# GpSimd's order in the batch turns: the first half's multiply ahead of the eight gathers of the next batch's second tile

## The chip, the cores and the metric

One core of a Trainium2 chip runs the whole program. The metric is device microseconds (us) of one execution; "before" is the median of three runs. The engines are TensorE (PE in the rows; PEld are its weight loads), VectorE (DVE), ScalarE (ACT), GpSimd (POOL) and SyncE (SP, which here only issues DMAs). Each runs its own instructions in order and waits on semaphores that the others raise.

## The reference, cut to what matters

Sixteen batches of 256 tokens of width 256 go through one decoder layer of three parts, each with a residual and a layer norm. Only the first two touch the change.

```python
# 1: memory of 8192 keys, top 8 per token
Q = x @ shared_compress[b];  scores = Q @ K.T / sqrt(128)
topk_scores, topk_idx = top_k(scores, 8);  weights = softmax(topk_scores)
x = layernorm(x + sum_k V[topk_idx[k]] * weights[k])
# 2: cross-attention, 16 heads of 64
q = x @ Wq;  k, v = split(context @ Wkv)
attn = softmax(clip(where(mask, q @ k.T / 8, -max), -5, 5))
x = layernorm(x + (attn @ v) @ Wo + bo)
# 3: routed feed-forward over groups of 32 tokens, once, after all batches
```

The eight rows V[topk_idx[k]] of 128 tokens (one tile) are fetched by eight gathers, one for each k. The softmax is divided late: attn @ v is made from unnormalised exponentials and multiplied by the inverse of the denominators.

## The kernel before, in words

All loops are written out at build time, so the order on each engine is fixed; `need(engine, semaphore, value)` is a wait. After a preamble the program goes through turns, `for c in TURNS`. Turn c does the attention of batch c (`cross`), the values V of batch m = c + 1 (`mid`), the scores against the keys of batches up to c + 2 (`score`, one block of 512 keys each, spread between everything else), and the output of batch p = c - 1 (`out`).

On TensorE a turn runs: the K projections (four jobs, `("K", c, j)`) with scores between them; the output product (`("WO", p, tile)`, `qT_heads` times `wo`); the transposes of x1 of tile 1; the Q projections; then, head pair by head pair, similarities (`sims`), `values` (`("PV", c, j)`, `exp` times `v`) and, after each half of the heads, `denominators` (`exp` times `head_selector`, into `den`). The turn ends with the four V projections of batch m (`("V", m, j)`, in the rows `side_bank<-wqkv_hi,ctx_hi` and its two companions), with a score block after each, and the transposes of x1 of tile 0 of batch m (line 548). The projection jobs use two PSUM banks in turn: a job needs the job two before it copied out by ScalarE (`heads_out`, line 927). I call the stretch from the first V matmul to the transposes of line 548 the V stretch.

The denominators of half h travel so: VectorE inverts `den` (`den_inverse`, line 1225), SyncE stores the result to DRAM (line 366 in the issue rows) and reads it back broadcast into `kT` (line 370, semaphore `rb_in0` or `rb_in1`), and GpSimd multiplies `qT_heads` (attn @ v of that half) by it: line 1446, semaphore `ot_done`. Two wait for that: ScalarE, before it copies the next batch's K jobs into `kT` (jobs 0 and 1 need the first half, 2 and 3 the second), and TensorE, before the output product (both).

On GpSimd a turn runs: small layer norm work, the gathers of tile 0 of batch m (five in a row, then one and two among the clips), the clips of `exp` (line 1425), and at its end the part that changes: gathers of tile 1 of batch m (`v_rows`, line 1397) and the two multiplies. VectorE sums the gathered rows of tile 1 (`value_sum`, line 1200) early in the next turn, before the transposes of x1 of tile 1.

Of the kernel before, what the change touches and what calls it, by code (L numbers as in the profile page):

```python
# [22 lines left out]
TOPK = 8  # L23
# [61 lines left out]
def build(nc, x, xT, xTs, ctxT, mcol, A, AT, BmT, WimpT, WrT, comp, KmT, V, Wq, Wk, Wv, Wo, bo, ctrl, f1, fb, f2,  # L85
# [4 lines left out]
    with ExitStack() as ctx:  # L90
        names = {}

        def sem(name):
            if name not in names:
                names[name] = ctx.enter_context(nc.semaphore(name))
            return names[name]
# [149 lines left out]
        def need(eng, name, v):  # L246
            if v > 0:
                eng.wait_ge(sem(name), v)
# [8 lines left out]
        def job_full(eng, key):  # L257
            need(eng, f"proj_full{JOB[key] % 2}", JOB[key] // 2 + 1)

        def job_done(eng, key):  # L260

            need(eng, f"proj_free{JOB[key] % 2}", JOB[key] // 2 + 1)
# [1114 lines left out]
        @block.gpsimd  # L1377
        def _(pool):

            for n in range(NK // KW):  # L1380
                pool.wait_ge(sem("k_hi"), n + 1)
                ks = slice(n * KW, (n + 1) * KW)
                nc.gpsimd.tensor_tensor(kl[:, ks], kraw[:, ks], kh[:, ks].bitcast(F32), ALU.subtract)\
                    .then_inc(sem("k_lo"), 1)

            pool.wait_ge(sem("main_ready"), 1)
            for n, (w, i, k) in enumerate(WCHUNKS):
                pool.wait_ge(sem("w_hi"), n + 1)
                nc.gpsimd.tensor_tensor(wl[:, i, k, :], wraw[:, 1, i, k, :], wh[:, i, k, :].bitcast(F32),
                                        ALU.subtract).then_inc(sem("w_lo"), 1)  # L1390

            def gather(batch, tile, ks):
                if ks[0] == 0:
                    need(pool, "sum_done", TT * batch + tile)
                    need(pool, "idx_done", TT * batch + tile + 1)
                for k in ks:
                    pool.indirect_dma_start(out=vg[:, k, :], out_offset=None, in_=V_rows,  # L1397
                                            in_offset=bass.IndirectOffsetOnAxis(ap=i8[:, tile, k:k + 1], axis=0))\
                        .then_inc(sem("vg_in"), 16)

            def rstd1(batch, tile):
                need(pool, "sum_done", TT * batch + tile + 1)
                nc.gpsimd.tensor_tensor(rs[:, tile:tile + 1], ve[:, tile:tile + 1], neghalf[:, 0:1], ALU.pow)\
                    .then_inc(sem("rstd1"), 1)

            for c in TURNS:
                m, a, p = c + 1, c + 2, c - 1
                cross, mid, out = (0 <= b < B for b in (c, m, p))
                if cross:
                    rstd1(c, 1)  # L1410
                    need(pool, "x1T_pe", TT * (c + 1))
                    for tile in range(TT):
                        last = nc.gpsimd.tensor_tensor(x1[c % 2][:, tile, :], x1[c % 2][:, tile, :], bob[:, :], ALU.add)
                    last.then_inc(sem("bo_done"), 1)
                if mid:
                    gather(m, 0, range(0, 5 if cross and m < B - 1 else TOPK))
                if out:
                    need(pool, "sum2_done", p + 1)
                    nc.gpsimd.tensor_tensor(rs2[:, :], ve2[:, :], neghalf[:, :], ALU.pow).then_inc(sem("rstd2"), 1)
                for h in range(H):  # L1420
                    if cross:
                        i = H * c + h
                        need(pool, "exp_done", i + 1)
                        for k in range(KT):
                            last = nc.gpsimd.tensor_scalar(ex[i % NEX][:, k, :], ex[i % NEX][:, k, :], ub[:, k, c:c + 1],  # L1425
                                                           E_LO, ALU.min, ALU.max)
                        last.then_inc(sem("clip_done"), 1)
                    if cross and m < B - 1 and h == 1:
                        gather(m, 0, (5,))
                    if cross and m < B - 1 and h == 3:  # L1430
                        gather(m, 0, (6, 7))
                    if mid and h == 5:
                        need(pool, "ctx_hi", m + 1)
                        nc.gpsimd.tensor_tensor(ctl[:, :, :], ct[:, :, :], cth[:, :, :].bitcast(F32), ALU.subtract)\
                            .then_inc(sem("ctx_lo"), 1)
                    if mid and h == 9:
                        rstd1(m, 0)
                if mid:
                    gather(m, 1, range(0, 5))
                for half in range(2):  # L1440
                    if cross and 2 * c + half < 2 * B - 1:
                        need(pool, f"rb_in{half}", 32 * (c + 1))
                        job_done(pool, ("PV", c, 2 * half))
                        job_done(pool, ("PV", c, 2 * half + 1))
                        hs = slice(4 * half, 4 * half + 4)
                        nc.gpsimd.tensor_tensor(qt[:, hs, :], qt[:, hs, :], kt[:, hs, :], ALU.mult)\  # L1446
                            .then_inc(sem("ot_done"), 1)
                    if mid and half == 0:
                        gather(m, 1, range(5, TOPK))


            job_full(pool, ("WO", B - 1, TT - 1))
            for j in range(NQ // 2):
                need(pool, "ffn2_pe", j - NF + 1)
                pool.dma_start(f1q[j % NF][:, :, :], f1[:, :, 2 * j * P:2 * (j + 1) * P]).then_inc(sem(f"fq_in{j % NF}"), 16)
                pool.dma_start(f2q[j % NF][:, :, :], f2_t[j]).then_inc(sem(f"fq_in{j % NF}"), 16)

            for n in range(NT):
                u = n % U
                need(pool, "aggr3", n + 1)  # L1460
                need(pool, "out_done", n - U + 1)
                nc.gpsimd.tensor_scalar(ve3[u][:, :], ag3[u][:, 1:2], EPS, None, ALU.add).then_inc(sem("var3"), 1)
                need(pool, "var3", n + 1)
                nc.gpsimd.tensor_tensor(rs3[u][:, :], ve3[u][:, :], neghalf[:, 0:1], ALU.pow).then_inc(sem("rstd3"), 1)
# [61 lines left out]
```

## Time and profile before

| | |
|---|---|
| time before, median of 3 runs (lowest to highest) | 1380.46 us (1378.34 to 1381.36) |
| the profiled execution: its time, its span | 1377.7 us, 1375.8 us |
| busy share of the span: PE, DVE, POOL, ACT | 96%, 82%, 53%, 52% |
| granted TensorE clock, mean | 0.99 |
| turns that change | those with `cross` and `mid`: c = 0 to 14 |

A turn takes some 69 us (the gathers at a turn's end start at 532.09, 601.19, 669.91 us). TensorE is busy nearly all the time, so the question for a change on GpSimd is where TensorE waits for something that comes from GpSimd's place in the order. The timeline rows below give for each instruction its start, its duration, engine, line, operation, result<-inputs, sizes, count, and in brackets the idle time before it and who ended it.

### The profile page before, as it was taken

The page shows a single profiled execution, that of the slowest core. Times are in us where ns is not written, and L with a number is a line of the kernel's source. Part 1 is how long each engine was busy: PE and PEld are TensorE (multiplying, and loading weights), DVE is VectorE, ACT ScalarE, POOL GpSimd, SP SyncE. Part 2 cuts the span into 40 slices and gives each one's busy share as a digit, 9 for nine tenths or more (in the row PEclk, how much of TensorE's full clock was granted, in tenths as well). Part 3 has the DMA queues.
Part 4 walks back from the last instruction along what each step waited for, and adds up shares of the span by engine and source line. Part 5 has one row for each costly group of instructions (what it writes and reads, how often), then busy time and mean ns, then how long its engine had stood idle before and what let it go on. Part 6 is the DMA issues. An engine that isn't in the chain of part 4 may idle for free.

```text
span 1375.8 us, 25304 instructions
## 1 busy us (share of the span) xinstructions
PE 1321.6 (96%) x9877; PEld 993.5 (72%) x9877; DVE 1125.4 (82%) x1628; ACT 718.8 (52%) x1377; POOL 728.9 (53%) x1009
## 2 busy tenths in 40 slices
PE   9877999999999999999999999999999999999898
PEld 5455778786878787878787868787878676767775
DVE  2479889898989898989898988898989986546567
ACT  1353655555555555555555555555555544336554
POOL 0554465555565656565655565656565647341434
PEclk9997999999999999999999999999999999999999
DMA  9562121212121212121212121212121216002412
GB/s 368 182 197 65 46 74 54 74 55 74 54 74 55 74 54 74 55 74 54 74 54 74 54 74 54 74 55 74 54 74 44 74 42 182 1 26 84 156 43 83
DMA packets 57557, 110.38 MB, mean 80 GB/s; under 512 B 9446, under 2 KB 38110, under 8 KB 56286
## 3 DMA queue, kind: packets, MB, share of 16 engines
q1 hardware_dynamic: 40350, 62.17, 15.0%
q0 software_dynamic: 14848, 41.96, 10.6%
q10 hardware_dynamic: 2240, 4.63, 0.9%
q8 instruction: 79, 1.29, 0.4%
q14 instruction: 40, 0.33, 0.1%
HBM read 98.50 MB, written 10.22 MB: 79 GB/s over the span
## 4 chain that ended last, share of the span: by engine, by line
PE 88%; DVE 5%; issue 2%; another core or an unknown queue 2%; ACT 2%; DMA 0%; SPq 0%; POOL 0%; POOLq 0%; ACTq 0%; DVEq 0%
PE side_bank L387 51%; PE score_bank L387 33%; PE score_bank L766 2%; DVE cand_idx L1177 1%; DVE cand_val L1174 1%; PE side_bank L766 1%; DVE dispatchedT L1335 1%; PE side_bank L548 1%; ACT exp L922 0%; PE score_bank L606 0%; ACT score_row L910 0%; SPq L318 0%; DVE x_sum L1200 0%; POOL exp L1425 0%
## 5 line engine op out<-in xcount | busy, mean ns | idle before, releaser
L910 ACT COPY score_row<-score_bank 128x512 f32<-128x512 f32 x512 | 298.9, 591 | 112.2 <-PE score_bank L387 56.7
L1397 POOL DMA_INDIRECT v_rows<-in_V,top_idx x256 | 249.0, 973 | 130.8 <-issue 74.5
L1174 DVE MAX8 cand_val<-score_row 128x8 f32<-128x2048 f32 x128 | 291.7, 2279 | 28.6 <-ACT score_row L910 26.3
L1177 DVE FIND_INDEX8 cand_idx<-cand_val,score_row 128x8 uint32<-128x2048 f32 x128 | 292.5, 2285 | 0.0
L1425 POOL TENSOR_SCALAR exp<-exp,exp_bound 128x256 f32<-128x256 f32 x512 | 248.9, 502 | 79.8 <-ACT exp L922 78.1
L387 PE MATMUL score_bank<-keysT_hi,qT_hi 128*128 128x512 f32 x512 | 216.9, 424 | 21.0 <-ACT score_row L910 19.9
L387 PE MATMUL score_bank<-keysT_hi,qT_lo 128*128 128x512 f32 x512 | 204.9, 400 | 0.0
L387 PE MATMUL score_bank<-keysT_lo,qT_hi 128*128 128x512 f32 x512 | 204.7, 400 | 0.0
L922 ACT ACTIVATE exp<-side_bank 128x512 f32<-128x512 f32 x256 | 139.1, 595 | 91.3 <-PE side_bank L387 84.3
L387 PE MATMUL side_bank<-qT_heads,kT 64*128 64x256 f32 x1024 | 145.2, 402 | 2.6 <-ACT exp L922 2.6
L387 PEld LDWEIGHTS score_bank<-keysT_hi,qT_hi 128*128 128x128 f32 x512 | 97.9, 191 | 62.1 <-ACT score_row L910 25.3
L1200 DVE SCALAR_TENSOR_TENSOR x_sum<-v_rows,top_weight,x_sum 128x256 f32<-128x256 f32 x256 | 134.2, 524 | 9.1
L927 ACT COPY qT_heads<-side_bank 128x512 f32<-128x512 f32 x128 | 75.2, 587 | 113.9 <-PE side_bank L387 91.9
L387 PE MATMUL side_bank<-exp,v 128*64 128x256 f32 x1024 | 125.5, 386 | 1.1 <-POOL exp L1425 1.0
L387 PEld LDWEIGHTS side_bank<-qT_heads,kT 64*128 64x128 f32 x1024 | 88.2, 186 | 51.5 <-issue 41.3
L387 PE MATMUL side_bank<-wo,qT_heads 128*128 128x256 f32 x512 | 115.8, 379 | 0.0
L387 PEld LDWEIGHTS score_bank<-keysT_hi,qT_lo 128*128 128x128 f32 x512 | 97.6, 191 | 23.9
L1446 POOL TENSOR_TENSOR qT_heads<-qT_heads,kT 128x1024 f32<-128x1024 f32 x31 | 74.4, 2399 | 71.2 <-DMA kT<-den_scratch 70.9
L387 PEld LDWEIGHTS score_bank<-keysT_lo,qT_hi 128*128 128x128 f32 x512 | 98.1, 192 | 15.7
L387 PEld LDWEIGHTS side_bank<-wo,qT_heads 128*128 128x128 f32 x512 | 96.7, 190 | 15.0 <-issue 1.2
L1225 DVE RECIPROCAL den_recip<-score_bank 128x256 f32<-128x256 f32 x32 | 56.0, 1749 | 60.4 <-remote 51.5
L387 PEld LDWEIGHTS side_bank<-exp,v 128*64 128x64 f32 x1024 | 67.4, 136 | 51.0 <-issue 20.9
(200 smaller groups left out, 2284.0 us busy)
## 6 DMA issues: line engine op xcount, KB each, us to landing
kT<-den_scratch SPq DMA_DIRECT2D x62, 256.0 KB
f_quads<-in_f POOLq DMA_DIRECT2D x32, 256.0 KB, 3.4
comp_then_wqkv_raw<-in_comp SPq DMA_DIRECT2D x6, 1024.0 KB, 19.0
xT_by_step<-in_xTs SPq DMA_DIRECT2D x4, 1024.0 KB, 9.1
xT_in<-in_xT SPq DMA_DIRECT2D x16, 256.0 KB
keysT_raw<-in_KmT ACTq DMA_DIRECT2D x8, 512.0 KB, 20.2
x_sum<-in_x SPq DMA_DIRECT2D x32, 128.0 KB, 2.0
ctxT_in<-in_ctxT SPq DMA_DIRECT2D x16, 256.0 KB
```

Source lines behind the costliest of these rows:

```text
L387: return nc.tensor.matmul(o, l, r, start=start, stop=stop, skip_group_check=True)
L766: last = nc.tensor.transpose(set2[n % 3][:, c0:c0 + P], dtt[:, n, k, :, g], idn[:, :])
L910: nc.scalar.copy(srow[n // PER % 2][:, i * CB:(i + 1) * CB], scb[n % 3]).then_inc(sem("score_evac"), 1)
L922: nc.scalar.activation(ex[i % NEX][:, :, :].rearrange("p k s -> p (k s)"), sp_[o][:, :], ACT.Exp, scale=A_SCALE).then_inc(sem("exp_done"), 1)
L927: nc.scalar.copy(to, job_bank(key)[:, :]).then_inc(free(key), 1)
L1174: own(nc.vector.max(cv[:, tile, cs], srow[g % 2][:, :]))
L1177: nc.vector.max_index(ci[:, tile, cs], cv[:, tile, cs], srow[g % 2][:, :]).then_inc(sem("cand_done"), 1)
L1200: own(nc.vector.scalar_tensor_tensor(acc[:, tile, :], vg[:, k, :], w8[:, tile, k:k + 1], acc[:, tile, :], ALU.mult, ALU.add))
L1225: nc.vector.reciprocal(rden[:, :], den).then_inc(sem("rden_done"), 1)
L1397: pool.indirect_dma_start(out=vg[:, k, :], out_offset=None, in_=V_rows, in_offset=bass.IndirectOffsetOnAxis(ap=i8[:, tile, k:k + 1], axis=0))\
L1425: last = nc.gpsimd.tensor_scalar(ex[i % NEX][:, k, :], ex[i % NEX][:, k, :], ub[:, k, c:c + 1], E_LO, ALU.min, ALU.max)
L1446: nc.gpsimd.tensor_tensor(qt[:, hs, :], qt[:, hs, :], kt[:, hs, :], ALU.mult)\
```

## The change

In turns with `cross` and `mid`, GpSimd ran five gathers of tile 1, the multiply of the first half, three gathers, the multiply of the second half. Now it runs the multiply of the first half, all eight gathers, the multiply of the second half. In the turn that has `mid` without `cross` (c = -1) the eight gathers stay in a row as they were.

```diff
@@ -1435,8 +1435,8 @@
                     if mid and h == 9:
                         rstd1(m, 0)
-                if mid:
-                    gather(m, 1, range(0, 5))
+                if mid and not cross:
+                    gather(m, 1, range(TOPK))
                 for half in range(2):
                     if cross and 2 * c + half < 2 * B - 1:
                         need(pool, f"rb_in{half}", 32 * (c + 1))
@@ -1445,8 +1445,8 @@
                         nc.gpsimd.tensor_tensor(qt[:, hs, :], qt[:, hs, :], kt[:, hs, :], ALU.mult)\
                             .then_inc(sem("ot_done"), 1)
-                    if mid and half == 0:
-                        gather(m, 1, range(5, TOPK))
+                    if mid and cross and half == 0:
+                        gather(m, 1, range(TOPK))
```

The end of turn 1 on GpSimd before, from the last clip on:

```order
103 L1425 TENSOR_SCALAR exp<-exp,exp_bound 128x256
104 L1397 DMA v_rows<-in_V,top_idx 128x256 [waits idx_done,sum_done]
105 L1397 DMA v_rows<-in_V,top_idx 128x256 x4
106 L1446 TENSOR_TENSOR qT_heads<-qT_heads,kT 128x1024 [waits proj_free1,proj_free0,rb_in0]
107 L1397 DMA v_rows<-in_V,top_idx 128x256 x3
108 L1446 TENSOR_TENSOR qT_heads<-qT_heads,kT 128x1024 [waits proj_free1,proj_free0,rb_in1]
109 L1403 TENSOR_TENSOR ln_rstd<-ln_var,neghalf 128x1 [waits sum_done]
```

And the same place of the changed kernel:

```order
102 L1425 TENSOR_SCALAR exp<-exp,exp_bound 128x256
103 L1446 TENSOR_TENSOR qT_heads<-qT_heads,kT 128x1024 [waits proj_free1,proj_free0,rb_in0]
104 L1397 DMA v_rows<-in_V,top_idx 128x256 [waits idx_done,sum_done]
105 L1397 DMA v_rows<-in_V,top_idx 128x256 x7
106 L1446 TENSOR_TENSOR qT_heads<-qT_heads,kT 128x1024 [waits proj_free1,proj_free0,rb_in1]
107 L1403 TENSOR_TENSOR ln_rstd<-ln_var,neghalf 128x1 [waits sum_done]
```

Five gathers moved from ahead of the first multiply, with its wait on `rb_in0`, to behind it; the other engines' orders are the same as before.

## Rows read from the trace of the kernel before

**Rows 1.** The page, the chain that ended last, by engine

```profile
PE 88%; DVE 5%; issue 2%; another core or an unknown queue 2%; ACT 2%; DMA 0%; SPq 0%; POOL 0%; POOLq 0%; ACTq 0%; DVEq 0%
```

**Rows 2.** Waits, whole run: total us, times, longest

```profile
PE side_bank L387 <- ACT v L927: 2.3, 3, 1.1
...
PEld side_bank L387 <- ACT v L927: 5.0, 7, 1.5
...
ACT v L927 <- remote: 69.1, 14, 6.0
...
DVE den_recip L1225 <- remote: 51.5, 15, 4.3
```

**Rows 3.** Timeline, TensorE: V stretch begins and ends, turns 0, 8, 13

```profile
192.16 0.50 PE L387 MATMUL side_bank<-wqkv_hi,ctx_hi 128*128 128x512 f32 x1
...
200.81 0.38 PE L548 MATMUL side_bank<-identity,x 128*128 128x128 f32 x2
...
742.34 0.50 PE L387 MATMUL side_bank<-wqkv_hi,ctx_hi 128*128 128x512 f32 x1
...
750.82 0.38 PE L548 MATMUL side_bank<-identity,x 128*128 128x128 f32 x2
...
1086.89 0.50 PE L387 MATMUL side_bank<-wqkv_hi,ctx_hi 128*128 128x512 f32 x1
...
1096.69 0.38 PE L548 MATMUL side_bank<-identity,x 128*128 128x128 f32 x2
```

**Rows 4.** Timeline, GpSimd, end of turn 6

```profile
601.19 1.03 POOL L1397 DMA_INDIRECT v_rows<-in_V,top_idx  x1 [0.16 <-issue]
...
606.30 0.96 POOL L1397 DMA_INDIRECT v_rows<-in_V,top_idx  x1 [0.30 <-issue]
607.28 2.40 POOL L1446 TENSOR_TENSOR qT_heads<-qT_heads,kT 128x1024 f32<-128x1024 f32 x1
...
612.41 0.96 POOL L1397 DMA_INDIRECT v_rows<-in_V,top_idx  x1 [0.30 <-issue]
619.02 2.40 POOL L1446 TENSOR_TENSOR qT_heads<-qT_heads,kT 128x1024 f32<-128x1024 f32 x1 [5.64 <-DMA kT<-den_scratch]
```

**Rows 5.** Turn 6: denominators on the chain, then timeline of VectorE, ScalarE

```profile
602.88 1.86 PE score_bank L387 x32
...
608.45 1.76 DVE L1225 RECIPROCAL den_recip<-score_bank 128x256 f32<-128x256 f32 x1 [3.16 <-remote]
...
608.52 0.59 ACT L927 COPY v<-side_bank 128x512 f32<-128x512 f32 x1 [5.00 <-remote]
```

**Rows 6.** Timeline, after the second multiply: ScalarE, VectorE, TensorE twice

```profile
621.45 0.59 ACT L927 COPY kT<-side_bank 128x512 f32<-128x512 f32 x1 [2.73 <-POOL qT_heads L1446]
...
621.47 4.13 DVE L1200 SCALAR_TENSOR_TENSOR x_sum<-v_rows,top_weight,x_sum 128x256 f32<-128x256 f32 x8
...
622.18 0.45 PE L387 MATMUL side_bank<-wo,qT_heads 128*128 128x256 f32 x1
...
630.55 0.27 PE L548 MATMUL side_bank<-identity,x 128*128 128x128 f32 x1
```

**Rows 7.** DMA queues within 599 to 605 us: packets, MB, share

```profile
q1 hardware_dynamic: 314, 0.66, 42.5%
q0 software_dynamic: 92, 0.26, 15.0%
```

**Rows 8.** Timeline, SyncE's issue of the second half's broadcast, turn 6

```profile
612.67 1.61 SPq L370 DMA_DIRECT2D kT<-den_scratch  x2
```

**Rows 9.** Turn -1, eight gathers in a row: GpSimd, TensorE, ScalarE

```profile
134.15 0.95 POOL L1397 DMA_INDIRECT v_rows<-in_V,top_idx  x1 [0.30 <-issue]
...
133.31 0.63 PE L387 MATMUL side_bank<-wqkv_hi,ctx_lo 128*128 128x512 f32 x1
...
133.98 0.59 ACT L927 COPY v<-side_bank 128x512 f32<-128x512 f32 x1 [1.97 <-PE side_bank L387]
```

**Rows 10.** Turn 14, beside the eight gathers of tile 0: ScalarE

```profile
1129.52 0.59 ACT L927 COPY qT_heads<-side_bank 128x512 f32<-128x512 f32 x1 [3.23 <-remote]
```

## The prediction

> **What bounds the kernel now.** I read the page's chain first: 88% of it is TensorE [rows 1]. So a change on GpSimd counts only where TensorE waits, and the next view is the list of waits. It has one entry at the place of the change: TensorE waits for ScalarE's copies of the V jobs, 2.3 us in three turns by its matmuls, 5.0 us in seven turns by its weight loads [rows 2]. Those copies themselves wait 69.1 us, and VectorE's inverse of the denominators 51.5 us, both with a releaser the profile cannot name ("remote") [rows 2].
>
> To price the entry I measured the V stretch of turns 0 to 13 in the timeline. It holds the same matmuls each time, so its shortest length is the one without a wait. In turn order the fourteen are 8.65, 8.48, 9.37, 8.47, 8.48, 8.47, 8.78, 8.64, 8.48, 9.34, 8.48, 8.66, 8.48 and 9.80 us; the rows show turns 0, 8 and 13 [rows 3]. The sum over 8.47 is 4.0 us, between the 2.3 and the 5.0 of the list of waits. Turn 14 has no scores in its V stretch, and no wait of TensorE on those copies; it is left out.
>
> Why the copies are late is seen in turn 6. The denominators' matmuls are over at 602.88 + 1.86 = 604.74 us, but VectorE, idle, starts the inverse at 608.45, and ScalarE starts the V copy at 608.52 [rows 5]. Two engines with different waits are let go together, 1.2 us after the fifth gather (606.30 + 0.96 = 607.26) [rows 4]. I found this distance, 1.1 to 1.3 us from the start of the first multiply to ScalarE's copy, in all fourteen turns from 0 to 13. So I take it that news of finished matmuls doesn't get through while this row of gathers runs. That is a reading of coincidence, not something a row states.
>
> **The change part by part.** Nothing is removed or added: eight gathers and two multiplies in each of 15 turns, in another order. In turn 6:
>
> 1. First multiply. The clips end at 601.0 (0.16 before the first gather) [rows 4]. It must then wait for its broadcast. The 512 KB broadcast and a 128 KB row load are 0.66 MB together, and the hardware queue had moved 0.66 MB by 605.0, even beside two gathers [rows 7]. So it runs by 605.0 to 607.4 (2.40 us) instead of 607.28 to 609.68. Behind its wait stand the gathers, for at most 4 us; they have no one who is waiting yet.
> 2. Denominators. They end at 604.74 with no gather issued. If my reading holds, VectorE inverts as soon as it is free, at about 605.3 (608.45 less its idle 3.16) to 607.1, instead of 608.45 to 610.21 [rows 5]. ScalarE copies V when its matmuls end. The wait of TensorE goes: 4.0 us in fourteen turns, bounds 2.3 and 5.0.
> 3. Gathers. From 607.6, spaced as before: five take 6.07 us from start to end, each further one 1.26, so eight take 9.9 and end at 617.5, where the last ended at 613.37 [rows 4]. That is 4.1 us later. What they serve is the sum on VectorE, which started at 621.47, and then the transposes of tile 1 at 630.55 [rows 6]. So the rows have 4.0 us to land before the sum would even start late, and from its start to the transposes are 9.1 us, of which it takes 4.13. No cost. If the cover were gone (a landing some 3 us after 621.5), each further us would hold the transposes by as much.
> 4. Second broadcast. The inverse was over at 610.21, the broadcast issued at 612.67, the multiply let go at 619.02: 2.46 and 6.35 us [rows 4, 5, 8]. From 607.1 on this gives 609.5 and 615.9. One or two more gathers share the engines than before; two cost 15.0% of 6 us, 0.45 us each [rows 7]. So 616.4 to 616.8, still ahead of the last gather.
> 5. Second multiply. Released by the gathers, not by the broadcast: 617.7 to 620.1, against 621.42 before. ScalarE's third K copy waited 2.73 us for it and ran at 621.45, and the output product came at 622.18 directly after the matmuls ahead of it [rows 6]. So there is no wait of TensorE to win there, but 1.3 us more room. What is late next is the gathers themselves, and they have that room.
> 6. After it, VectorE is about 1 to 2 us ahead at the start of each turn. It is not what TensorE waits for, so I count 0 (0 to 0.6 us over the run).
>
> Sum: 0 - 4.0 + 0 + 0 + 0 - 0 = -4.0 us, bounds -2.3 and -5.6. Against the profiled execution (1377.7 us, span 1375.8) that is 1373.7. That execution is 2.8 us faster than the median of the runs shown, 1380.46; taken from the median the sum gives 1376.5 us (1374.9 to 1378.2).
>
> The worst point is 2 together with 3: now eight gathers run in a row beside the V and K projections. The nearest rows are the eight gathers of turn -1, also beside V jobs. There the copy started at 133.98, 0.04 us after its matmuls (133.31 + 0.63), with seven gathers of the row issued and the eighth about to be, at 134.15 [rows 9]. That speaks for no late news with these matmuls. Against it stand the eight gathers of turn 14 beside the similarities: ScalarE waited 3.23 us, again "remote" [rows 10]. The similarities and the denominators are matmuls over a part of the array, and the V and K projections use all of it (128*128). In all cases where the news was late a part-array matmul came first; I rest on that.
>
> The Trainium skill, page "SBUF — State Buffer", section "Who interferes with whom", says that only VectorE and GpSimd contend, that TensorE and ScalarE never wait on anyone, and that DMA contends with no compute engine. By that rule gathers can't hold back ScalarE's copy, what holds it is something else that the change leaves in place, and the sum would be 0 instead of -4.0.
>
> **The rivals.**
>
> A. The forecast: late releases in the V stretch go. 1376.5 us. Chance 0.60.
>
> B. The change doesn't do what it could: what lets VectorE and ScalarE go late hangs on the denominators' matmuls or on something else at that place, and moves with them. For it: the releaser is unnamed, and in turns 9 and 13 VectorE was let go before ScalarE, not together with it. Against it: the fixed distance to the fifth gather. Then TensorE waits as before, 1380.5 us. Chance 0.25.
>
> C. Slower: the longer row of gathers delays news of the V and K matmuls too. If it is held from 3.6 us into the row (604.74 against 601.19 in turn 6) to 1.2 us after it, that is 611.2 to 618.7. TensorE has two banks, so it would run on until the first K job, which needs the third V copy: about 9.1 us into the V stretch, 613.8. It would stand until 618.7 and a copy of 0.59 us, 5 us a turn, 14 turns: 70 us, 1450 us. If only one copy in a turn is late by the 1.2 us seen after a row, 17 us: 1397 us. It decides from 0.29 us a turn (4.0 / 14). For it speaks the late copy of turn 14 [rows 10], against it the prompt one of turn -1 [rows 9]. Chance 0.13.
>
> The remaining 0.02 is for a gather or broadcast that lands too late (steps 3 and 4).
>
> **How the numbers follow.** A and B hold 0.85. A's own range is 1374.9 to 1378.2, with 1.5 us on each side for a median of runs that lie 3 us apart: 1373.5 to 1379.5. B with the same 1.5 us reaches 1382. The range 1373.5 to 1382 leaves out C and a little of A. A difference of 0.2% is 2.8 us, about what a measurement of this kernel can tell from no change: A gives 0.54 for faster and 0.06 for same, B 0.25 for same, C 0.13 for slower, the rest 0.02 slower.
>
> **What would show it.** Right: VectorE's inverse and the V copies no longer wait for "remote" at a turn's end; V stretches all near 8.47 us; the first multiply waits for its broadcast and the second directly follows the eighth gather; no wait of ScalarE's K copy on GpSimd, or one under 1 us. Wrong: TensorE waiting for copies of V or K jobs beside the eight gathers (C), or the inverse still 3 us late with no gather before it (B). The weakest step is 2, the cause of the late release.

## The result and the profile after

| | before | after |
|---|---|---|
| median of six runs each, us (lowest to highest) | 1378.39 (1375.81 to 1381.36) | 1393.4 (1389.54 to 1397.8) |
| ratio, 95% interval | | 1.0108 (1.009 to 1.0126) |
| profiled execution: time, span, us | 1377.7, 1375.8 | 1391.56, 1389.7 |

The change makes the kernel 1.1% slower. Three more runs of the kernel before bring its median from 1380.46 to 1378.39 us. The span of the profiled executions grew by 13.9 us. The page's chain of work that ended last, by engine, for the changed kernel; the share of TensorE was 88% in [rows 1], ScalarE's 2%:

```profile
PE 85%; DVE 5%; ACT 3%; another core or an unknown queue 3%; issue 2%; DMA 0%; SPq 0%; POOL 0%; POOLq 0%; ACTq 0%; DVEq 0%
```

The waits of the whole run, in the columns of [rows 2]: total us, times, longest us.

```profile
ACT v L927 <- PE side_bank L387: 70.1, 52, 2.9
...
ACT kT L927 <- remote: 48.4, 15, 4.4
...
DVE den_recip L1225 <- PE score_bank L387: 17.8, 14, 5.4
...
PEld side_bank L387 <- ACT kT L927: 13.9, 10, 1.9
...
PE side_bank L387 <- ACT kT L927: 9.7, 9, 1.5
...
PEld side_bank L387 <- ACT exp L922: 6.2, 11, 0.6
```

The two entries that the change was to remove are gone: neither the V copies nor VectorE's inverse waits for "remote" any more. In their place the K copies do, 48.4 us in 15 times, and TensorE waits for them. I call the stretch from the transposes of line 548 to the first matmul of the output product the K stretch, and that from the first shared q matmul (`xT_in,sc_in`) to the first `exp,v` matmul the q stretch. Measured in the timeline as the V stretch was:

| sum over the turns, us | before | after | difference |
|---|---|---|---|
| V stretches, 14 turns (shortest 8.47 and 8.49) | 122.6 | 118.9 | -3.7 |
| K stretches, 14 turns (shortest 8.72 and 8.73; after, up to 10.49) | 122.4 | 135.5 | +13.1 |
| q stretches, turns 1 to 13 (shortest 6.08) | 79.7 | 81.6 | +2.0 |
| the rest between turn 0's V stretch and turn 14's | | | -0.8 |
| ahead of turn 0's V stretch; from turn 14's on | | | -1.1; +4.4 |

Turn 6 shows the whole course. Timeline of GpSimd:

```profile
607.61 2.39 POOL L1446 TENSOR_TENSOR qT_heads<-qT_heads,kT 128x1024 f32<-128x1024 f32 x1 [3.44 <-DMA kT<-den_scratch]
610.16 1.05 POOL L1397 DMA_INDIRECT v_rows<-in_V,top_idx  x1 [0.16 <-issue]
...
619.10 0.96 POOL L1397 DMA_INDIRECT v_rows<-in_V,top_idx  x1 [0.30 <-issue]
620.08 2.38 POOL L1446 TENSOR_TENSOR qT_heads<-qT_heads,kT 128x1024 f32<-128x1024 f32 x1
```

VectorE and ScalarE in the same turn:

```profile
608.34 1.74 DVE L1225 RECIPROCAL den_recip<-score_bank 128x256 f32<-128x256 f32 x1
...
609.76 0.59 ACT L927 COPY v<-side_bank 128x512 f32<-128x512 f32 x1 [2.85 <-PE side_bank L387]
...
617.65 0.37 ACT L914 CAST x1T_hi<-side_bank 128x256 fp32r<-128x256 f32 x1 [0.30 <-PE side_bank L548]
...
622.00 0.59 ACT L927 COPY kT<-side_bank 128x512 f32<-128x512 f32 x1 [3.98 <-remote]
```

And TensorE:

```profile
608.07 0.50 PE L387 MATMUL side_bank<-wqkv_hi,ctx_hi 128*128 128x512 f32 x1
...
616.56 0.38 PE L548 MATMUL side_bank<-identity,x 128*128 128x128 f32 x2
...
618.09 0.28 PE L387 MATMUL side_bank<-ctx_hi,wqkv_lo 128*128 128x256 f32 x1
...
622.64 0.39 PE L387 MATMUL side_bank<-ctx_hi,wqkv_hi 128*128 128x256 f32 x1 [1.44 <-ACT kT L927]
...
626.99 3.61 PE L387 MATMUL side_bank<-wo,qT_heads 128*128 128x256 f32 x16
```

The inverse starts 0.3 us into the V stretch, and up to 6.0 us into the row of gathers ScalarE copies each V job within 0.2 us of its matmuls' end. The copy of the transposes at 617.65 already starts 0.7 us behind them (616.56 + 0.38 = 616.94). Then the first K job's matmuls are over at 618.09 + 0.28 = 618.37 us, but its copy starts at 622.00: 1.9 us behind the last gather (619.10 + 0.96 = 620.06). The third K job needs its bank and stands until 622.64, 1.44 us. The K stretch takes 626.99 - 616.56 = 10.4 us instead of 8.7. In the order of before the row of five had ended early in the V stretch (607.26 us in turn 6 [rows 4]), and in the row of three behind it no V or K copy was late.

The trace also holds the time of each semaphore update, from which the views tell a releaser ("remote": the update is there, but no instruction that makes it ended just before). In this turn four groups of matmuls are over at 618.37, 619.07, 620.50 and 621.20 us; their updates come at 621.92, 621.97, 622.10 and 622.15. In the same turn of the kernel before, with the row of five, ends at 604.75, 606.34, 607.04 and 608.44 us have updates at 608.42, 608.50, 608.55 and 608.62. So it isn't ScalarE or VectorE that wakes late: TensorE's updates themselves come late and in one burst. Some updates of these stretches are missing from the record, so nothing is said here of those of other engines. This is what "news" means below.

How far into a row this begins differs. With the row of five ahead of the first multiply, a job that was over 2.4 us after the first gather was held (turn 13); in the rows of eight of the changed kernel none before 6.2 us. Of the fifteen late K copies eleven start 1.6 to 1.9 us behind the last gather and four within 0.3 us of it.

Turn 14 has the same in another place. TensorE, then ScalarE, then the last two of the eight gathers; the row began at 1171.20:

```profile
1181.84 1.10 PE L387 MATMUL score_bank<-x2T_pair,controller 128*128 128x256 f32 x4 [2.56 <-issue]
```

```profile
1181.15 0.59 ACT L934 COPY x2T_pair<-score_bank 128x512 f32<-128x512 f32 x1 [2.96 <-remote]
```

```profile
1178.84 0.95 POOL L1397 DMA_INDIRECT v_rows<-in_V,top_idx  x1 [0.30 <-issue]
1180.09 0.95 POOL L1397 DMA_INDIRECT v_rows<-in_V,top_idx  x1 [0.30 <-issue]
```

Behind the stand of 2.56 us TensorE is slower for a while. Its granted clock was 1.00 (2.4 GHz) up to 1182.9 us and 0.50 (1.2 GHz) from 1184 to 1186, where the 128x256 matmuls take 0.41 us instead of 0.28; from 1187 on it is 1.00 again. From the transposes of line 548 to the output product turn 14 takes 14.19 us instead of 9.85, which is nearly all of the +4.4 at the end of the table.

### The profile page after: what moved, and what is told of

Its sections match the earlier page's. It is cut to its first block, busy times and chain, and to the rows that moved or that the text cites. A ratio compares the mean times of both kernels' runs of the same rounds, so it can differ in the third digit from the quotient of the medians.

```text
span 1389.7 us, 25304 instructions
## 1 busy us (share of the span) xinstructions
PE 1323.9 (95%) x9877; PEld 994.1 (72%) x9877; DVE 1112.0 (80%) x1628; ACT 721.4 (52%) x1377; POOL 726.7 (52%) x1009
## 3 DMA queue, kind: packets, MB, share of 16 engines
q0 software_dynamic: 14848, 41.96, 10.4%
## 4 chain that ended last, share of the span: by engine, by line
PE 85%; DVE 5%; ACT 3%; another core or an unknown queue 3%; issue 2%; DMA 0%; SPq 0%; POOL 0%; POOLq 0%; ACTq 0%; DVEq 0%
PE side_bank L387 49%; PE score_bank L387 32%; PE score_bank L766 2%; DVE cand_idx L1177 1%; DVE cand_val L1174 1%; ACT exp L922 1%; PE side_bank L766 1%; DVE dispatchedT L1335 1%; ACT score_row L910 1%; PE side_bank L548 1%; PE score_bank L606 0%; ACT kT L927 0%; SPq L318 0%; ACT v L927 0%
## 5 line engine op out<-in xcount | busy, mean ns | idle before, releaser
L927 ACT COPY qT_heads<-side_bank 128x512 f32<-128x512 f32 x128 | 75.2, 587 | 103.6 <-PE side_bank L387 92.1
L387 PE MATMUL side_bank<-ctx_hi,wqkv_hi 128*128 128x256 f32 x256 | 76.0, 297 | 10.7 <-ACT kT L927 9.7
```

The source lines that it names most:

```text
L387: return nc.tensor.matmul(o, l, r, start=start, stop=stop, skip_group_check=True)
L927: nc.scalar.copy(to, job_bank(key)[:, :]).then_inc(free(key), 1)
```

## The experiments

The eighteen runs fell on six chips; each group below that shares a chip says so. The kernel before had medians of 1377.8 to 1379.0 us on five of them (on one it is a single run) and 1370.6 on the sixth, so a time is read beside its own chip's. Theories: **T**, news of finished matmuls is held only once a plain-float32 matmul (the transposes) has run beside the gathers; **P**, only part-array matmuls or transposes cause it; **L**, the length of an unbroken row of gathers does it, with **L1** (any compute instruction of GpSimd ends a row) and **L2** (the gathers must pause for about a microsecond); **H**, a broadcast into `kT` beside the gathers does it; **N**, the number of gathers in the last 10 us does.

**First group, one chip (before: 1378.18 us).** The transposes moved ahead of the V jobs, on TensorE and in ScalarE's copies:

```diff
+                if mid:
+                    x1_transpose(m, 0)
                 for j in range(4):
                     if mid:
                         key, tile, hf = ("V", m, j), j // 2, j % 2
...
-                if mid:
-                    x1_transpose(m, 0)
```

> The changed kernel, with the transposes of x1 of tile 0 (line 548) and ScalarE's copy of them moved from behind the V projections to ahead of them, so that between the first of the eight gathers and 1.7 us after the last TensorE runs only projections and scores. Theory T (news of finished matmuls is held back only once a matmul on plain float32 operands has run beside a row of gathers; the transposes are the first such matmul, 6 us into the row): the late K copies go (the 48.4 us in 15 times of ScalarE's K copy behind 'remote' falls under 10), the 13 us of longer K stretches go, time 1377 to 1380 us. Rival L (the length of the row alone holds the news back from its fifth or sixth gather on, whatever matmul runs): K copies as late as before this edit, time 1390 to 1396 us.

Measured 1388.74 us, ratio 1.0082 (1.0062 to 1.0102). Waits:

```profile
ACT kT L927 <- remote: 31.6, 11, 4.7
```

With the transposes over before the row begins, K copies are late eleven times, in ten turns, instead of fifteen times in fourteen turns. T wanted almost none, so the transposes aren't the condition; L wanted them as late as before, and the time is 1.3 us under its range. Why fewer turns are hit I can't say.

Five gathers between the multiplies and three behind the second:

```diff
-                    if mid and cross and half == 0:
-                        gather(m, 1, range(TOPK))
+                    if mid and cross:
+                        gather(m, 1, range(0, 5) if half == 0 else range(5, TOPK))
```

> The changed kernel, but five of the eight gathers between the two multiplies and three behind the second. The row of five starts 2 us into the V stretch and ends at about 8 us, before the transposes; the three run beside the K projections. Theory T: no late news, or only that of the transposes and first K copy for under 1 us; K stretch under 8.9 us; time 1375 to 1380 us. Rival L: rows of five were held up before (the V copies), so the copies of the fourth V job are late from 3.6 us into the row, V or K stretch longer by up to 1 us, time 1380 to 1390 us.

Measured 1400.05 us, ratio 1.0152 (1.0122 to 1.0183). The V stretches are all 8.49 us and the K stretches all 8.73: cutting the row at the same place, beside the same matmuls, took away the whole +13.1. That is against L as it was put here, which had V or K copies late from 3.6 us into a row of five; and the time is above both forecasts. A new wait appears, ahead of the Q projections:

```profile
DVE x_sum L1200 <- DMA v_rows<-in_V,top_idx: 62.5, 15, 5.2
...
PEld side_bank L387 <- DVE x1T_lo L1218: 22.4, 14, 2.4
```

The second multiply waits for its broadcast, the three gathers wait behind it, and the sum of the rows comes so late that the transposes of tile 1 and the Q projections stand, 18.2 us in 14 turns. It is the case that step 3 of the prediction had priced as "if the cover were gone".

Two plain-float32 matmuls behind the third V job, and as a control the same two with fp32r operands; they write a bank that the next score block overwrites, so the output is that of the changed kernel:

```diff
+                    if cross and mid and j == 2:
+                        for _ in range(KT):
+                            mm(sp_[1][:, 0:P], idn[:, :], idn[:, :])
```

> The changed kernel with two extra full-array 128x128 matmuls on plain float32 operands (identity times identity, into an unused bank) in each turn behind the third V job and its scores, 6.3 us into the V stretch and 4.2 us into the row of gathers. They add 0.2 us a turn by themselves. Theory T: from them on the news is held back, so the copy of the fourth V job (in time until now) becomes late in nearly all turns by 3 us or more, and TensorE waits longer: K stretch longer by 1 to 2 us a turn, time 1405 to 1420 us. Rival P (only matmuls over a part of the array or transposes start it): as the changed kernel, 1391 to 1397 us. Rival L: as the changed kernel too.

> The same two extra matmuls at the same place, but on float32r operands (weights of the projection times themselves), as the control. Theory T: no effect beyond 0.1 to 0.2 us a turn; fourth V copy in time, 1391 to 1398 us. If the extra matmuls as such are what matters, it equals the run with the float32 ones.

One run each: 1403.45 and 1394.85 us. The waits of the run with float32:

```profile
ACT v L930 <- PE side_bank L387: 84.6, 59, 2.9
...
ACT kT L930 <- remote: 46.0, 14, 5.4
```

No V copy waits for "remote" with a float32 matmul two jobs ahead of it and gathers all around. The K copies wait as in the changed kernel (46.0, and 47.8 us in the control). The V stretch is longer by the dummies themselves, 0.44 and 0.22 us; over 14 turns the first is 6 us, most of what puts 1403.45 above the forecasts of P and L. T has fallen. P isn't touched by these two runs; against it stands the first of this group, where the row of eight and what followed it had neither transposes nor part-array matmuls beside them until the copies were late.

**Second group, another chip (before: 1378.54 us).** Now the order of before with a shorter first row:

```diff
                 if mid:
-                    gather(m, 1, range(0, 5))
+                    gather(m, 1, range(0, 3))
...
-                        gather(m, 1, range(5, TOPK))
+                        gather(m, 1, range(3, TOPK))
```

> The order of before with three gathers of tile 1 ahead of the first multiply instead of five, and five behind it. Theory L (an unbroken row of GpSimd gathers holds back the news of finished matmuls from some 5 us into the row until 1.2 to 1.9 us behind its end, whatever matmuls run; a break by a multiply lets it through): the row of three ends before the denominators do, the inverse and the V copies go on time, V stretches all 8.48 us; the row of five behind the multiply holds nothing that TensorE waits for (the run with five gathers between the multiplies showed none in the V and K stretches), K stretches 8.73; 1374.5 to 1377.5 us. Theory H (the transfer of a broadcast into kT beside the gathers holds the news): the first half's broadcast still runs beside gathers, V stretches as before, 1377 to 1380 us.

The same with four and four:

> The order of before with four gathers ahead of the first multiply and four behind it. L: the row of four ends 1.2 us earlier than that of five, so the inverse and the V copy go some 1.2 us earlier or on time; of the 4.0 us that TensorE lost in the V stretches at most 1 stays, K stretches 8.73; 1374.5 to 1377.5 us. H: as before, 1377 to 1380 us.

Measured 1376.31 us, ratio 0.9986 (0.9976 to 0.9996), and 1375.66 us, ratio 0.998 (0.9971 to 0.999). In both all V stretches are 8.49 and all K stretches 8.73 us. The waits for the inverse, first with three ahead, then with four:

```profile
DVE den_recip L1225 <- PE score_bank L387: 25.3, 17, 5.1
```

```profile
DVE den_recip L1225 <- remote: 37.4, 15, 4.3
```

With four the inverse is still late (51.5 us in [rows 2]), but let go early enough that the V copies don't cost TensorE anything. So what the change was to win could be had by moving one or two gathers instead of five, and H doesn't fit: the broadcast still lies beside gathers. Both gain less than the 4.0 us, since the q stretches are longer by 2.0 and 1.8 us (more on them below).

The changed kernel without the broadcast of the second half:

```diff
-                        for o in range(2):
+                        for o in range(2 - 2 * h):
...
-                        need(pool, f"rb_in{half}", 32 * (c + 1))
+                        if half == 0:
+                            need(pool, f"rb_in{half}", 32 * (c + 1))
```

> The changed kernel without the broadcast of the second half's inverse into kT, and without GpSimd's wait for it; the second multiply then takes what stands in kT, so that the division of the second half is left out. The eight gathers stay in a row beside the V and K matmuls, as in turn -1, which has no broadcast and no late copy. L: nothing changes, ScalarE's K copies wait 40 to 50 us for remote, 1390 to 1395 us. H: the K copies are on time (under 10 us for remote), K stretches 8.73, 1377 to 1381 us.

One run, 1393.64 us; `ACT kT L927 <- remote` 43.4 us in 13 times, K stretches up to 10.66 us. H has fallen: the late K copies need no broadcast.

Six gathers between the multiplies, two behind:

> The changed kernel with six gathers between the two multiplies and two behind the second. L, with news held from about 5.5 us into a row: the row of six lasts 7.3 us and ends at 615, so at most the third V copy or a score copy is late, V stretches up to 9 us, K stretches 8.73; the two gathers behind the second multiply end about 1.3 us earlier than the three of the run with five between, and part of its 15 us before the Q projections stays: 1385 to 1396 us. H: K copies late as in the changed kernel, and the wait before the Q projections too: over 1400 us.

One run, 1383.08 us. V 8.49, K 8.73 in every turn: a row of six in that place still costs TensorE nothing (two K copies are late, 6.1 us), and of the wait ahead of the Q projections 4.4 us are left. The stretches are as L has them; the time is 1.9 us under its range.

**Third group, another chip (before: 1379.01 us).** The changed kernel with one tiny copy in the middle of the row:

```diff
+        spare = sb(main, "spare", [P, 1])
...
-                        gather(m, 1, range(TOPK))
+                        gather(m, 1, range(0, 4))
+                        nc.gpsimd.tensor_copy(spare[:, :], neghalf[:, 0:1])
+                        gather(m, 1, range(4, TOPK))
```

> The changed kernel with one small GpSimd copy (128x1) of a constant into a spare tile between the fourth and the fifth of the eight gathers; nothing else differs. Theory L1: any GpSimd compute instruction ends the row and lets the news through, so the row of eight becomes two of four: V stretches 8.49, K stretches 8.73, ScalarE's K copies wait under 10 us for remote, 1377 to 1381 us. Theory L2: it takes a pause of the gathers of a microsecond or more (as behind every row so far, 1.2 to 1.9 us from its end to the late copies), so a copy of a fraction of a microsecond changes nothing: K copies wait 40 to 50 us for remote, 1389 to 1395 us.

Measured 1390.19 us, ratio 1.0096 (1.0062 to 1.013); K copies wait 47.9 us in 16 times for "remote". L1 has fallen: a compute instruction as such doesn't end a row.

Four and four, and tile 0's row cut as well:

```diff
-                    gather(m, 0, range(0, 5 if cross and m < B - 1 else TOPK))
+                    gather(m, 0, range(0, 4 if cross and m < B - 1 else TOPK))
...
-                        gather(m, 0, (5,))
+                        gather(m, 0, (4, 5))
```

> The run with four gathers ahead of the first multiply and four behind it, and in turns 0 to 13 also the row of five gathers of tile 0, beside the first similarities, cut to four: the fifth goes behind the second head's clip with the sixth. L (either form): late copies beside the row of five cost 0.2 us a turn in the stretch from the Q projections to the first values (6.08 us at its shortest, 6.3 in most turns); they go in nearly all turns, 2 to 2.7 us less than the run with four and four, 1372 to 1375 us. If the length of the row is not what holds the news, that stretch stays at 6.3 us in most turns and the time at 1375 to 1376.5 us.

Measured 1371.61 us, ratio 0.9953 (0.9938 to 0.9968): 0.5% faster than the kernel before beside it, and 0.4 us under L's range. Thirteen turns, counted from V stretch to V stretch, take 68.53 us each, with no stretch over its shortest; the q stretches are all 6.08 us. The news isn't always in time even so: the inverse waits 36.0 us for "remote" in 14 times beside the row of four, at no cost to TensorE.

**Fourth group, another chip (before: 1377.81 us).** Six and twelve tiny copies in the place of the one, into a spare tile of 12 columns:

> The changed kernel with six of the small copies, one behind the other, between the fourth and the fifth gather, a pause of 0.4 to 1.2 us (one took 0.20 us). L2 (held news gets through once the gathers pause for a microsecond or so): part of the K stretches is near 8.73, the sum of their excess over 8.73 (13.4 us in the changed kernel, 16.8 with one copy) falls to 3 to 10 us; 1379 to 1388 us. L1 (any break does) has fallen. Theory N, a rival: the pause has nothing to do with it and only the number of gathers in the last 10 us counts: excess of the K stretches as with one copy, 12 to 17 us, 1387 to 1393 us.

> Twelve small copies in the same place, a pause of 0.8 to 2.4 us. L2: K copies on time but for those that wait for the second multiply, which now runs up to 2.4 us later (some 622.5 instead of 620.1 in turn 6; the third K copy can wait up to 1 us for it): the excess of the K stretches falls under 4 us, none of it by remote; 1376 to 1382 us. N: excess 12 us or more as before, 1387 to 1395 us.

One run each: 1372.09 and 1369.53 us, with `ACT kT L928 <- remote` at 18.1 us in 8 times and 1.6 us in one; the pauses were 0.78 and 1.48 us. The late copies fit L2, but both times lie some 7 us under its ranges: the shortest stretches had changed too (V 8.43, K 8.52), and the wider tile had moved what lies behind it. Two things had changed at once.

**Fifth group, another chip (before: 1370.58 us)**, to tell these apart. One copy with the wide spare tile; the kernel before with that tile unused; twelve copies timed; the best order with that tile unused:

> The changed kernel with one small copy between the fourth and the fifth gather, as in the first run of this kind, but with the spare tile 12 columns wide as in the runs with six and twelve copies, so that all tiles behind it lie where they lay there. If the pause is what freed the K copies: they are late as with one copy (40 to 50 us for remote, K stretches 10 to 17 us in excess), 1382 to 1391 us. Theory A, that the place of the tiles in SBUF did it: K copies on time, 1369 to 1373 us.

> The kernel before, with the unused spare tile of 12 columns in the place it has in the other runs, and no other change. It gives what the moved tiles are worth by themselves: the shortest stretches were 8.43, 8.52, 11.30 and 8.24 us with six and twelve copies against 8.49, 8.73, 11.34 and 8.34 before. If the place does that, some 0.4 us a turn and 1371 to 1375 us; if not, 1378 to 1380 us.

> The changed kernel with twelve small copies once more, timed. By its one look 1369 to 1371 us, 0.5 to 0.7% under the kernel before.

> The kernel with four and four gathers of tile 1, and tile 0's row cut to four (1371.6 us), with the spare tile of 12 columns and no copies. If the two effects add up: 1371.6 less 4 to 6 us for the shorter stretches, 1365 to 1368 us. If the place of the tiles does nothing: 1371 to 1373 us.

Measured, in that order: 1365.43 us, ratio 0.9961 (0.9945 to 0.9976); 1363.77 us, 0.9949 (0.9934 to 0.9964); 1373.15 us, 1.0017 (1.0008 to 1.0027); 1364.33 us, 0.9955 (0.9942 to 0.9969). The waits of the second of them, the order of before:

```profile
ACT v L928 <- PE side_bank L388: 77.3, 64, 2.9
...
ACT kT L928 <- PE side_bank L388: 52.0, 63, 0.9
...
DVE den_recip L1226 <- PE score_bank L388: 27.9, 14, 5.4
```

On this chip there is no wait for "remote" in any of the four runs, beside rows of five or of eight; V copies, K copies and inverse go when their matmuls end. None of TensorE's 1219 semaphore updates in any of these four traces comes more than 0.12 us behind its matmuls. The expectation that copies would be late with one small copy missed, and the twelve copies took 1373 us instead of 1369 to 1371; but the fourth group had the wide tile and late copies, so it isn't the tile.

Either the chip differs, or something of the one session in which all four ran; the unpadded kernel before, 7 to 8 us faster here than on the other five, fits a chip without held news, but it left no trace here. The gathers keep the same pace, 1.28 us from start to start on either kind of chip. Where no news is held the new order has nothing to win: with one copy it is 1.7 us slower than the order of before with the same tile (1365.43 against 1363.77).

What the tile itself does is a price of its own: -6.8 us against the kernel before beside it. The mean matmul is shorter; groups by shape, before (the first trace, of another chip) and then with the tile (busy us, mean ns):

```profile
L387 PE MATMUL side_bank<-ctx_hi,wqkv_hi 128*128 128x256 f32 x256 | 74.0, 289 | 0.0
...
L387 PE MATMUL side_bank<-wqkv_hi,ctx_hi 128*128 128x512 f32 x128 | 53.5, 418 | 2.3 <-ACT v L927 2.3
```

```profile
L388 PE MATMUL side_bank<-ctx_hi,wqkv_hi 128*128 128x256 f32 x256 | 72.6, 284 | 0.0
...
L388 PE MATMUL side_bank<-wqkv_hi,ctx_hi 128*128 128x512 f32 x128 | 51.7, 404 | 0.0
```

The 418 ns are of a kernel with late V copies; in the two orders of four and four, without the tile, it is 407 and 411. An undisturbed turn takes 68.08 us with the tile and 68.53 without; 14 turns of 0.45 are 6.3 of the 6.8. The shortest K stretch was 8.51 or 8.52 in all runs with the wide tile (three chips) and 8.72 or 8.73 in all others that have a turn without a late K copy, so this goes with the place of the tiles. Why another place makes these matmuls shorter isn't shown. And twelve copies cost here: with no news to free, they only make the second multiply late.

**Last pair, a sixth chip (before: 1378.57 us).** One and twelve copies, same tiles, same chip:

> The same kernel as pad_filler (one copy, spare tile of 12 columns), now side by side with the one of twelve copies on one chip. On a chip on which the rows of gathers hold the news: K copies late for remote by 40 to 50 us, K stretches 10 to 17 us in excess of 8.52, some 1380 to 1386 us with the kernel before at 1378. On a chip like that of pad_before and pad_filler, where not one wait for remote is left: 1365 us, with the kernel before at 1370.6, and nothing is told of the pause.

> The kernel of filler12 and filler12b again. On a chip that holds the news, if the pause of 1.48 us frees it: remote waits of the K copies under 5 us, K stretches under 4 us in excess, 1369 to 1375 us, and 8 us or more under the one with one copy. If the pause does nothing, both have the same time within 3 us and the same late copies. On the other kind of chip 1373 us, for the late second multiply.

Measured 1390.51 us, ratio 1.0097 (1.0068 to 1.0126), and 1375.49 us, ratio 0.9977 (0.9966 to 0.9988). Waits with one copy, and turn 6 on GpSimd and ScalarE:

```profile
ACT kT L928 <- remote: 43.9, 18, 3.9
```

```profile
607.61 1.05 POOL L1398 DMA_INDIRECT v_rows<-in_V,top_idx  x1 [0.16 <-issue]
...
612.46 0.20 POOL L1452 COPY spare<-neghalf 128x1 f32<-128x1 f32 x1
...
616.60 0.95 POOL L1398 DMA_INDIRECT v_rows<-in_V,top_idx  x1 [0.30 <-issue]
```

```profile
619.06 0.59 ACT L928 COPY kT<-side_bank 128x512 f32<-128x512 f32 x1 [0.96 <-remote]
```

The same with twelve:

```profile
ACT kT L928 <- POOL qT_heads L1447: 40.3, 15, 4.1
...
PE side_bank L388 <- ACT kT L928: 3.3, 3, 1.3
```

```profile
605.41 1.05 POOL L1398 DMA_INDIRECT v_rows<-in_V,top_idx  x1 [0.16 <-issue]
...
610.26 1.49 POOL L1452 COPY spare<-neghalf 128x1 f32<-128x1 f32 x12
...
615.71 0.95 POOL L1398 DMA_INDIRECT v_rows<-in_V,top_idx  x1 [0.30 <-issue]
```

```profile
613.74 0.59 ACT L928 COPY kT<-side_bank 128x512 f32<-128x512 f32 x1 [0.84 <-issue]
```

The eleven copies, and with them the pause, are the only difference. At 0.20 us the K copies are late for "remote" in 18 cases; at 1.49 us in none, and what they wait for is the second multiply, which TensorE hardly feels (3.3 us). The medians differ by 15.0 us; of the 8.8 us between the two traces (with one copy it is the fastest of four runs) the K stretches are 6.1, their excess over 8.52 falling from 9.4 to 3.3 us. Both times lie above their forecasts, by 4.5 and 0.5 us.

L2 stands. N has fallen as it was put, with an excess of 12 us or more, but isn't excluded: the starts of the eight gathers lie 10.3 us apart with twelve copies (605.41 to 615.71) and 9.0 with one, so the pause also brings the number in any 10 us from eight to seven.

The program with one copy is also that of the fifth group: 43.9 us of late K copies here, none there. Of TensorE's semaphore updates 49 come over 1 us late here, up to 4.3 us.

## Why the prediction was wrong, point by point

- **Step 1 (first multiply earlier)**: right. In turn 6 it waits 3.44 us for its broadcast, and no engine stands for the gathers behind it.
- **Step 2 (the late release in the V stretch goes, -4.0 us)**: right, -3.7 us. Rival B fell with it.
- **"I rest on that" (only part-array matmuls start late news; V and K projections are safe)**: this is the step that failed. It let step 3 put the longer row of gathers into the sum at 0; measured, it is +13.1 us in the K stretches. The K projections use the whole array and their news is held all the same. The dummy matmuls and the moved transposes speak against the kind of matmul as the condition. What the runs show is the length of the unbroken row: six in a row, and five, cost TensorE nothing in that place, eight cost 13.1 us; four, a pause of 1.49 us and four cost 3.3 us.
- Why the evidence misled: rows of five had the denominators in them (though the late V copy of [rows 5] itself waits for a whole-array job), and the row of eight in turn -1 was judged by one copy [rows 9]. That copy shows that news can still pass with seven gathers issued; it doesn't show that it always does. In the changed kernel too every V copy passes, and in turn 6 the first late one comes 8.2 us into the row (618.37 against 610.16). The late copy of turn 14 [rows 10] was the better witness and I explained it away.
- **Rival C** is what happened, in its light form: it gave 1397 us for one copy late by 1.2 us a turn. Measured: the K stretches are 0.94 us a turn longer (13.1 over 14), 1393.4 us. Its deciding point, 0.29 us a turn, was passed threefold. Its heavy form, 5 us a turn, assumed that the news is held from 3.6 us into the row; it is held later, so the V jobs go free.
- **Step 3, as far as the landing of the gathers goes**: right. The room was smaller than it looked: the runs with five or six gathers between the multiplies show the price of using it up, 18.2 and 4.4 us.
- **Steps 4 and 5 (second broadcast, second multiply behind the gathers)**: right (620.08, directly behind the eighth), and as said worth nothing.
- **Step 6 (VectorE ahead: 0 to -0.6 us)**: wrong sign. Tile 0's row of five now starts earlier against the similarities (7.07 instead of 6.06 us ahead of the shared q matmuls in turn 7), and copies are held there: +2.0 us in the q stretches. Cutting this row to four, in the order of four and four, brings every q stretch back to 6.08 us. I had not gone past the change to the next row of gathers. The first gather of that row and the first of those matmuls, before, then after:

```profile
635.86 1.02 POOL L1397 DMA_INDIRECT v_rows<-in_V,top_idx  x1 [3.41 <-DVE top_idx L1190]
```

```profile
641.92 1.02 PE L387 MATMUL side_bank<-xT_in,sc_in 128*128 128x256 f32 x4
```

```profile
639.60 1.02 POOL L1397 DMA_INDIRECT v_rows<-in_V,top_idx  x1 [2.40 <-DVE top_idx L1190]
```

```profile
646.67 1.02 PE L387 MATMUL side_bank<-xT_in,sc_in 128*128 128x256 f32 x4
```

- Turn 14 on: +4.4 us, a stand of 2.56 us for another late copy beside eight gathers and, behind it, some three microseconds at half the clock. The prediction left this turn out.
- That the time fell near rival C's 1397 us is in part luck: C had one copy late by 1.2 us in each turn; the K stretches cost 0.94 us a turn, and the rest comes from places that no rival named.

The Trainium skill, page "SBUF — State Buffer", section "Who interferes with whom", has TensorE and ScalarE wait on no one and DMA contend with no compute engine; it speaks of ports to SBUF. The trace agrees as far as those go: the late copy itself takes its 0.59 us. But the sum of 0 that the prediction drew from it doesn't come out. On the chips where the news is held, ScalarE starts late beside a row of gathers, by an idle time of 3.98 us in turn 6, and taking the gathers away from the denominators did win 3.7 us.

What stays open: by what path gathers hold TensorE's semaphore updates; whether it is time or their number since the last pause that counts; why it began 2.4 us into a row of five and not before 6.2 us into a row of eight; why one chip, or one session, doesn't show it. The length of pause that is needed lies between 0.20 and 1.49 us; 0.78 us (six copies, 18.1 us of late K copies left) was in between, on a chip of its own.

## What to carry to other kernels

Don't let GpSimd issue long rows of indirect gathers beside matmuls whose results another engine is to fetch at once. In this kernel rows of four with a multiply between them cost TensorE nothing, though they too held an inverse back; a break of 1.49 us in a row of eight was enough, one of 0.20 us wasn't. Before moving such a row, look at what it will lie beside, there and at the next row, and take every late start for "remote" near gathers as a sign, however many prompt ones there are. Where the profile names no releaser, compare the semaphore's update with the end of the instruction that makes it. Test a pause and a place in memory apart from each other, and both on more than one chip.

## What the runs showed of the hardware that I had not expected

- A completed matmul's news reached ScalarE 3.6 us late (618.37 to 622.00) beside a row of eight gathers, 1.9 us behind the row's end. The semaphore updates of four groups of matmuls that had ended over 2.8 us came within 0.23 us.
- It isn't there on every chip or in every session: no such wait in four runs on one chip, where the kernel before took 1370.6 us instead of 1377.8 to 1379.0. One and the same program had 43.9 us of late K copies on one chip and none on that one.
- After a stand of 2.56 us TensorE's granted clock was 0.50 for some three microseconds (turn 14 of the changed kernel).
- A spare tile of 48 bytes a partition, never used, made the kernel 6.8 us (0.5%) faster on that chip: an undisturbed turn takes 68.08 us with it and 68.53 in traces without, the 512-column V matmul 404 ns in the mean instead of 407 to 418.
- The best order found (four and four, and four for tile 0) with the spare tile was run only on that chip, where it equals the padded order of before (1364.33 and 1363.77 us). On the others an estimate from these two runs is 1371.6 - 6.8 = 1365 us; no run shows it.
